# The step before the expert tiles of a two-layer attention and mixture-of-experts kernel: last batch's normalised rows on ScalarE, its statistics in two parts, two experts' weights sent between tile loads

## The reference

```
x = x + _L0_xattn_ref(_layernorm(x), ctx, ctx, ...)     # 16 heads, distance bias
x = x + _L0_ffn_ref(_layernorm(x), ...)                 # product keys, top 8, plus dense silu
x = x + _L1_xattn_ref(_layernorm(x), ctx, ctx, ...)     # 16 heads, relu projections
x = x + _L1_ffn_ref(_layernorm(x), ...)                 # below

def _L1_ffn_ref(x, ln_gamma, ln_beta, gate_w, w1, w2):  # E = 8 experts, K = 2, C = 256, F = 512
    mu, var = mean(xf), var(xf)
    rn = (xf - mu) * rsqrt(var + EPS) * ln_gamma + ln_beta
    probs = softmax(rn @ gate_w.T)
    rw, sel = top_k(probs, K)
    comb = sum(one_hot(sel, E) * rw[..., None], axis=1)
    h = gelu(einsum('nc,efc->enf', xf, w1))
    y = einsum('enf,ecf->enc', h, w2)
    return einsum('enc,ne->nc', y, comb)
```

## Time and profile before

| what | us |
|---|---|
| median of 3 runs | 1135.71 |
| lowest, highest | 1132.48, 1136.11 |
| profiled execution, its own time | 1129.27 |
| its span in the trace | 1127.5 |
| PE busy | 1001.2 (89%) |
| DVE busy | 783.4 (69%) |
| ACT busy | 652.5 (58%) |
| POOL busy | 497.7 (44%) |

### The profile page before, as it was taken

The page is one execution under the profiler, slowest core; times in us unless marked ns, Lnnn a source line. Parts: engine busy times, 40 slices in busy tenths (PEclk is TensorE's granted clock), DMA queues, the critical chain, the costliest instruction groups (busy, mean ns, idle before and its releaser), DMA issues.

```text
span 1127.5 us, 17009 instructions
## 1 busy us (share of the span) xinstructions
PE 1001.2 (89%) x5550; PEld 633.1 (56%) x5550; DVE 783.4 (69%) x1755; ACT 652.5 (58%) x874; POOL 497.7 (44%) x550
## 2 busy tenths in 40 slices
PE   8789999989778989989999779899998887999991
PEld 3345444434466778778777564344443333888881
DVE  7767688887888787787787346788888845344443
ACT  3356667666566766676677434576675560555550
POOL 6458898896415434433543342115051435122220
PEclk9899999999999999999999999999999889999996
DMA  8754979648999600000002231376554328222226
GB/s 245 224 171 161 289 194 354 192 156 267 230 220 217 124 1 1 1 2 0 1 6 74 62 104 54 112 209 150 149 148 121 96 81 342 62 70 71 71 62 224
DMA packets 74201, 149.89 MB, mean 133 GB/s; under 512 B 7823, under 2 KB 44577, under 8 KB 72580
## 3 DMA queue, kind: packets, MB, share of 16 engines
q1 hardware_dynamic: 61380, 98.80, 34.0%
q0 software_dynamic: 10800, 47.63, 11.9%
q10 hardware_dynamic: 1936, 2.36, 0.6%
HBM read 73.14 MB, written 76.25 MB: 133 GB/s over the span
## 4 chain that ended last, share of the span: by engine, by line
PE 63%; DVE 14%; ACT 10%; issue 5%; DMA 3%; POOL 3%; SPq 1%; ACTq 0%; DVEq 0%; POOLq 0%
PE ps L1313 15%; PE ps L1447 10%; PE ps L1428 7%; PE ps L1413 5%; PE ps L1387 4%; PE ps L1397 3%; PE ps L1655 3%; ACT pt L1105 3%; PE ps L1618 3%; PE ps L1632 3%; DVE negmax L1852 2%; PE ps L1776 2%; PE ps L1456 2%; PE ps L1331 1%; DVE moe_w L2198 1%
## 5 line engine op out<-in xcount | busy, mean ns | idle before, releaser
L1852 DVE TENSOR_REDUCE negmax<-ps 128x2 f32<-128x1024 f32 x256 | 309.7, 1222 | 60.2 <-PE ps L1413 58.2
L1105 ACT ACTIVATE pt<-ps 128x1024 f32<-128x1024 f32 x256 | 259.2, 1027 | 137.4 <-PE ps L1428 135.6
L1447 PE MATMUL ps<-pt,v_aug 128*32 128x512 f32 x1024 | 145.4, 634 | 3.9 <-POOL pt L804 3.1
L1428 PE MATMUL ps<-sq,sk 57*128 57x512 f32 (+1 forms) x512 | 129.2, 503 | 6.8 <-DMA sq<-m_sb 3.9
L1413 PE MATMUL ps<-sk,sq 56*128 56x512 f32 (+1 forms) x512 | 108.5, 429 | 18.8 <-ACT pt L1105 15.0
L804 POOL TENSOR_TENSOR pt<-pt,near 128x256 f32<-128x256 f32 x128 | 92.5, 730 | 51.0 <-ACT pt L1105 50.4
L1428 PEld LDWEIGHTS ps<-sq,sk 57*128 57x128 f32 (+1 forms) x512 | 49.4, 190 | 109.1 <-issue 71.0
L996 POOL DMA_INDIRECT expert_out<-yo,dest x39 | 38.1, 977 | 116.4 <-ACT yo L1280 101.7
L908 POOL TENSOR_TENSOR w_first<-w_first,moe_w 128x1024 f32<-128x1024 f32 x16 | 38.1, 2380 | 104.4 <-DVE pt L2190 103.6
L1618 PE MATMUL ps<-sel,hl 128*128 128x512 f32 x256 | 72.3, 415 | 5.1 <-DVE pt L2190 5.1
L1413 PEld LDWEIGHTS ps<-sk,sq 56*128 56x128 f32 (+1 forms) x512 | 50.5, 194 | 40.5 <-ACT pt L1105 28.4
(11 more groups left out here) (323 smaller groups left out, 2059.5 us busy)
## 6 DMA issues: line engine op xcount, KB each, us to landing
expert_rows<-zero SPq DMA_DIRECT2D x3, 5586.0 KB, 61.7
expert_weights_split<-wst POOLq DMA_DIRECT2D x8, 2048.0 KB, 8.5
qk_rows<-hl SPq DMA_DIRECT2D x30, 512.0 KB, 3.1
sk<-qk_rows SPq DMA_DIRECT2D x62, 192.0 KB, 5.0
sq<-qk_rows SPq DMA_DIRECT2D x62, 192.0 KB, 4.5
moe_w<-in_w POOLq DMA_DIRECT2D x16, 512.0 KB, 7.7
wexp<-expert_weights_split POOLq DMA_DIRECT2D x16, 512.0 KB, 4.8
wexp<-expert_weights_split SPq DMA_DIRECT2D x4, 2048.0 KB, 16.7
```

Source lines behind the costliest of these rows:

```text
L1105: act.activation(pt[:, 4 * (U % 2) + 2 * half:4 * (U % 2) + 2 * half + 2, :], ps[:, bank:bank + 2, :], ACT.Exp, scale=(BIAS, SCALE)[L]).th ...
L1428: ins = pe.matmul(ps[:, key.bank + s, :], sk[r, pair, c * P:(c + 1) * P], sq[r, pair, :], start=True, stop=True)
L1447: ins = pe.matmul(ps[32 * j:32 * j + 32, OBANK, :], v_aug[:, b % 2, c, HG * g + j, :], pt[:, 4 * (U % 2) + j, :], start=(c == 0), stop=(c ...
L1852: dve.tensor_reduce(negmax[:, n % 2, col:col + 9:8], ps[:, job.bank:job.bank + 2, :], AX, ALU.max, negate=True).then_inc(s_jd, 1)
```

## The change

Six edits.

1. In every batch `pick16`, which PE's ranking waits for, is made before the two small copies to `pay`, not after them.
2. For the last batch `gate_weights` stands in step 78, ahead of the places, and no longer in step 79 behind them.
3. The last batch's statistics are taken in two parts: 192 of 256 channels in step 64, once POOL has added the third group, and the last 64 channels where all 256 were. `bn_aggr` joins both.
4. The last batch's normalised rows are written by ACT (an activation with scale and bias per row) and not by POOL. DVE makes the bias, minus mean times inverse root, in `nb3`.
5. SP loads the weights of experts 4 and 5 where it loaded 4 to 7. Those of experts 6 and 7 go in quarters of 512 KB, two ahead of each of the row loads of tiles 3 to 6. The first row number is read before the wait for the sends.
6. PE's 14 filler products before the tiles become 12, then a wait for all sends, then 2.

```
             for e in (4, 5):
                 sp.dma_start(wexp[:, (ME - 1 - e) * EW:(ME - e) * EW].bitcast(F32), wx[e]).then_inc(s_wx[e], 16)
             sp.wait_ge(s_tile, 1)
-            for i in range(2):
-                sp.wait_ge(s_sent[i], 16 * 2 * TT * 2)
             for j in range(NTILE):
                 row = sp.value_load(tile_row[0:1, j:j + 1], min_val=0, max_val=XROWS - P)
+                if j == 0:
+                    for i in range(2):
+                        sp.wait_ge(s_sent[i], 16 * 2 * TT * 2)
+                if 3 <= j < 7:
+                    last_expert(6 + (j - 3) // 2, range(2) if j % 2 else range(2, 4))
                 if j >= 3:
...
                 if b == B - 1:
-                    norm3(b)
                     send_rows(b, range(TT))
...
+                        act.wait_ge(s_nb, 1)
+                        act.wait_ge(s_sent[(B - 1) % 2], 16 * 2 * TT)
+                        for t in range(TT):
+                            act.activation(pay[:, (B - 1) % 2, t, 0:D], x_tok[:, B - 1, t, :], ACT.Identity,
+                                           bias=nb3[:, t:t + 1], scale=rs3[:, 0, t:t + 1]).then_inc(s_ln3, 1)
...
-            keep_busy(14)
+            keep_busy(12)
+            for i in range(2):
+                pe.wait_ge(s_sent[i], 16 * 2 * TT * 2)
+            keep_busy(2)
...
+                    if L == 1 and U == LASTU:
+                        dve.wait_ge(s_res, NG * B - 1)
+                        stats_of(0, 64 * (NG - 1), 0, range(TT))
...
-                        if part == 12:
+                        if part == (11 if b == B - 1 else 12):
                             gate_weights(b)
...
                 for i in range(2):
                     own(dve.tensor_tensor(pick[:, i], per_e(col("expert")), per_t(two_e[:, i, :]), ALU.is_equal))
+                own.wait()
+                dve.tensor_tensor(pick16[:], pick[:, 0], pick[:, 1], ALU.add).then_inc(s_pick, 1)
+                if b == B - 1:
+                    dve.scalar_tensor_tensor(out=nb3[:], in0=mv3[:, :, 0], scalar=-1.0, in1=rs3[:, 0, :], op0=ALU.mult, op1=ALU.mult).then_inc(s_nb, 1)
                 if b >= 2:
                     dve.wait_ge(s_sent[b % 2], 16 * 2 * TT)
                 own(dve.tensor_copy(pay[:, b % 2, :, D + ME + 1], two_e[:, 0, :]))
                 own(dve.tensor_copy(pay[:, b % 2, :, D + ME], col("token")[:, TT * b:TT * (b + 1)]))
-                own.wait()
-                dve.tensor_tensor(pick16[:], pick[:, 0], pick[:, 1], ALU.add).then_inc(s_pick, 1)
```

More of the change, by code:

```diff
@@ L1761, in up @@
                 if j < ME:
-                    pe.wait_ge(s_wx[j], 16 if j >= 4 else 64)
+                    pe.wait_ge(s_wx[j], 16 if j in (4, 5) else 64)
                 pe.wait_ge(s_xl, j + 1)
@@ L1955, in attention @@
                             dve.wait_ge(s_res, NG * (b + 1))
-                            stats(0, x_tok[:, b], range(2 * part, 2 * part + 2))
+                            if b < B - 1:
+                                stats(0, x_tok[:, b], range(2 * part, 2 * part + 2))
+                            else:
+                                stats_of(64 * (NG - 1), D, 1, range(2 * part, 2 * part + 2))
                         if part == 1:
@@ L2043, in first_norm, with stats_of @@
                                       ALU.subtract, ALU.mult).then_inc(s_ln0, 1)
+            def stats_of(c0, c1, piece, blocks):
+                for t in blocks:
+                    own(dve.bn_stats(last6[:, t, piece, :], x_tok[:, B - 1, t, c0:c1]))
             def ln3_variance(b):
@@ L2047, in ln3_variance @@
                     dve.wait_ge(s_ln3, TT * b)
-                moments(0, mv3)
+                if b < B - 1:
+                    moments(0, mv3)
+                else:
+                    own.wait()
+                    for t in range(TT):
+                        own(dve.bn_aggr(mv3[:, t, :], last6[:, t].rearrange("p i s -> p (i s)")))
+                    own.wait()
                 own(dve.tensor_copy(vv[:, 0, :], mv3[:, :, 1]))
```

13 lines of the change are left out of this document (11 added, 2 removed).

## The result

| | before | after |
|---|---|---|
| median, us | 1135.74 (6 runs, 1132.48 to 1137.04) | 1126.65 (6 runs, 1120.38 to 1128.37) |
| ratio, 95% interval | | 0.9917 (0.9891 to 0.9943) |
| profiled execution, us (span) | 1129.27 (1127.5) | 1126.24 (1124.4) |
| granted clock, mean, profiled execution | 0.955 | 0.958 |

The two profiled executions are only 3.0 us apart. The median of before is 6.4 above its profiled execution, that of after 0.4 above its own. So there are two questions: what became of the terms on the path (5.0 forecast, 3.0 seen in the profiles), and where the other 6 us of the medians come from.

A forecast was written before the change was run, and what follows sets the result against it. PE's chain bounds, with a 32 us break between attention and tiles where one batch is finished, sent and fetched. 0.8 + 1.8 + 0.8 - 0.7 + 2.3 = 5.0 us; 1135.7 - 5.0 = 1130.7, range 1127.5 to 1134.0.

The forecast's parts named there:

- Tying the profiled execution to the median: Whole run: the median was 6.4 above the profiled 1129.27 us, and the like was expected of the changed kernel.
- `pick16` first, batches 0 to 2 (0.8): PE's waits for picks: `pick16`, held beside POOL's add, gains 0.28 us three times, 0.8 (0 to 2.2).
- First tiles' clock (2.3 won): First up products and the turn between: PE, busy from 952.5, regains full clock in time; 2.3 us won.
- Last two fillers (0.7 lost): After the sends land: two fillers take 3.00 us at half clock and delay the first turn; 0.7 lost (0 to 1.0).
- the clock does not come back: Rival, first tiles: fillers and first up products run at half clock; only 2.7 us gained, 1133.0 us; 22%.
- Last batch (1.8): Last batch, gate products to sends: faster DVE work and ACT's rows start the sends 1.8 us earlier (1.4 to 2.2).
- DVE's part: Last batch: norm off POOL ends DVE's stretched instructions, 1.45 us; `pick16` ahead of the two copies, 0.17.
- The weights' 0.6: Last batch: gate weights move into DVE's wait for PE's ranking, bringing row numbers 0.6 us earlier (0.4 to 0.6).
- ScalarE's duration: Last batch: four normalised rows on ACT take 2.0 us and, instead of DVE's row numbers, release the sends.
- SP (0.8 won): Last send to first row load: reading the row number before the wait saves 0.8 us (0.5 to 0.9).
- Weights between tiles: Experts 6 and 7's weights, sent between tile loads, land in about 5 us and cost nothing.
- Statistics in two parts: Last batch on DVE: at most 1.06 us goes, but costed at nothing since DVE waits for PE's gate products.

The follow-up runs named there:

- B: Comparison of kernels run on one chip beside the kernel before, testing addresses, repetition and fillers; before there: 1136.04 us, mean clock 0.9478.
- C: Comparison of kernels run on one chip beside the kernel before, testing which edit has the clock; before there: 1135.72 us, mean clock 0.947.
- a1: Kernel before with only `pick16` moved ahead of the two payload copies, in all four batches: 1131.36 us, ratio 1.0018.
- c3: Kernel before with only `pick16` ahead of the two copies in all batches, run again in another comparison: 1125.54 us, ratio 0.9920.
- b4: Changed kernel with the 14 fillers before the tiles in one go, as before: 1128.39 us, ratio 0.9941 to the kernel before.
- a2: Kernel before with only the last batch's normalised rows made by ScalarE (`nb3` added): 1134.45 us, ratio 1.0034.
- e1: Kernel before unaltered, run for a second profile: 1130.07 us, ratio 1.0015.
- d4: Changed kernel with one filler instead of three in the last ranking's step and one instead of two behind the last send: 1125.97 us, ratio 0.9920 to before.
- b1: Kernel before with one unused tile of 16 bytes per partition that shifts later addresses: 1134.65 us, ratio 1.0009.
- b2: Changed kernel with its two new tiles declared behind `dest`, so all others keep their old addresses: 1124.58 us, ratio 0.9895 to the kernel before.
- d2: Kernel before with `pick16` ahead of the two copies in batches 0, 2 and 3, not in batch 1: 1127.34 us, ratio 0.9933.
- e2: Kernel before with `pick16` ahead of the two copies in batch 0 alone: 1133.48 us, ratio 1.0036.
- c2: Changed kernel with `pick16` behind the two copies again in batches 0 to 2: 1136.44 us, ratio 1.0004 to the kernel before.
- A: Comparison of kernels run on one chip beside the kernel before, testing single parts of the change; before there: 1130.31 us, mean clock 0.9561.
- E: Comparison with the kernel before run once more and batch 0 alone; before there: 1129.32 us, mean clock 0.957, 2 of 23 executions under 0.950.
- a3: Kernel before with one unread product on PE ahead of its wait for the picks of batches 0 to 2: 1126.59 us, ratio 0.9962.
- c4: Changed kernel with new tiles behind `dest`, an unread product before batches 0 to 2's pick waits, and one filler for three and for two: 1119.88 us.
- d3: Kernel before with one unread product on PE ahead of its wait for batch 1's picks, nothing moved: 1125.69 us, ratio 0.9910.

## Why the prediction was wrong, step by step

**Tying the profiled execution to the median.** This step failed. Behind it lies a term that the sum does not have at all, the clock that PE loses behind batch 1's picks (next point). I made the sum against the profiled execution, found the median 6.4 us above it and expected the like of the changed kernel. The offset was no constant: after, it is 0.4. Three executions at 1132.48 to 1136.11 us beside a profiled one of 1129.27 say that the profile showed a luckier execution than most, and the fit says in what: 6.6 us for each 0.01 of granted clock. At equal clock after is 2.3 us faster than the before beside it in B and 0.9 in C, 2.0 with all comparisons pooled (1128.3 against 1130.2); the other 6 to 7 us of the medians are clock.

**`pick16` first, batches 0 to 2 (0.8).** On the path the term was right: PE stands 1.08, 1.08 and 1.33 us instead of 1.36, 1.35 and 1.60, 0.28 + 0.27 + 0.27 = 0.8 won. Whole runs can't resolve it: the same edit is worth 0.3 at equal clock in a1 and 2.3 in c3. What the step left out is that the half level followed batch 1's standstill in the profile of before, for ten us and 3.0 us of time. I read the clock only around the break. A view of the clock by stretch over the 100 us ahead of the first tile would have shown 0.50 from 872 to 882. The choice of 0.28 us a batch, against 0.7 with `pick16` not held, was my estimate from L2096 and L2080, and it was borne out (0.61 us for `pick16` beside POOL's add, 0.27 won); what the edit was worth lay beside it.

**First tiles' clock (2.3 won).** This term was wrong: the first up product takes 2.92 to 2.94, as before, in every kernel here, with 14 fillers together, 12 and 2, or 12 and 1. **Last two fillers (0.7 lost).** They take 3.75 us at a granted clock of 0.50, from 949.38 to 953.13, after PE idled 3.38, and the first turn comes 1.06 later than with 14 in one go (b4). I had read 3.00 for two at half clock, but the granted clock of that stretch, 927.34 to 930.34, is 0.59: the last part of them ran at the full level. The rival "the clock does not come back" was right about both. Its number for the profiled execution, 2.7 gained, is near the measured 3.0 by accident: 3.0 are batch 1's clock, 1.8 were there ahead of any changed instruction, 0.8 are the earlier picks and 0.3 the rest of the attention, 1.5 were lost in the break and 1.3 at the end.

**Last batch (1.8).** DVE's part is right against the profile that it was made from: 1.45 + 0.17 = 1.62 forecast from `gz` to `pick16`, 4.33 - 2.69 = 1.64 measured (1.48 in a2). Beside e1 it is 0.83: there only the shift of the four instructions is stretched (0.54), and product, cast and picks take 0.20, 0.17 and 0.29 with nothing changed and POOL's four instructions beside them. So the exact agreement is partly luck. The weights' 0.6 came too: 0.61 from the ranking to the row numbers. What was won ahead of the ranking was given back there, where it starts 2.08 behind `pick16` instead of 0.33 (1.10 in e1). I took it as following the picks, but DVE is now earlier than the three fillers that PE has ahead of it, and they run mostly at half clock (5.12 us at 0.55): the bound passed from DVE to PE. With one filler there it is 0.34 (d4). ScalarE's duration was right (2.07 for 2.0), but with the row numbers that late it is not what releases the sends.

**SP (0.8 won).** Right: 0.23 from landing to issue, 0.2 forecast. In after it is hidden behind the two fillers, since the turn waits for these. **Weights between tiles.** Right: never waited for; 4.9 us to landing, and a tile every 3.6 us in both. **Statistics in two parts.** At nothing, as forecast: DVE waits 3.29 us for PE's gate products.

**Left out: the addresses.** Two new tiles move all that are declared behind them. The results' fetching then lands in 7.8 instead of 6.8 us, and with eight of them one behind another the end is 1.3 longer; b1 and b2 put it at 1.4 and 1.7 at equal clock. The change would have been that much better with the tiles declared last, as b2 was.

**Open.** Why the half level lasts 10 us in one execution and 31 in another after the same standstill, what in batches 0, 2 and 3 kept d2 out of the lower group (e2 does not answer it), and why before meets it in four executions of five in one hour and hardly ever in another. There is no long stretch in a profile of before itself, only in c2's; that its lower group is the same thing is likely from the clock and not shown. The changed kernel was never run in an hour like A or E. From the levels at equal clock I would expect 1 to 2 us there and not 9 (an estimate); no run shows it.

## To carry to other kernels

Before an edit is summed on the critical path, list the granted clock by stretch over the whole kernel and look at each place where it falls behind a standstill of PE: in some hours a few tenths of a us on such a wait were worth 8 to 10 us and in others nothing, and one unread product in it did as much as the whole change. Compare the profiled execution with the other times of the same kernel before the sum is tied to either, and where they are apart, forecast each with its own clock. A second profile of the kernel before costs little and shows which of its pieces are clock. Declare new on-chip tiles behind the existing ones (ahead of them they cost 1.4 and 1.7 us at equal clock here), and after taking time from one engine in a chain, look again at what fills the time of the next one, since fillers placed for the old timing can become the bound (here the ranking began 2.08 us behind `pick16` instead of 0.33).

## What the runs showed of the hardware

- PE's standstills of 1.35 to 1.38 us for batch 1's picks were followed by the half clock (0.50) in six of eight profiles, for 3 to 31 us, those of 1.08 to 1.10 in one of nine. For batch 0's picks it followed 1.36 and 1.08 us alike, in all 18 profiles. The length of the standstill does not decide alone. A product that filled the wait kept the full clock behind it in all three profiles (batch 1: a3, c4, d3) and both (batch 0: a3, c4).
- The mean granted clock varied from 0.939 to 0.967 between the executions of the fit, at 6.6 us for each 0.01. The same kernel on the same chip had medians of 1135.72 and 1129.32 us in two comparisons.
- In ten us of the results' fetching, loads of 512 KB into `wexp`, the DMA engines moved 384 GB/s in before and 351 in b1, which differs only by an unused tile of 16 bytes per partition declared ahead of it, at a busy share of 1.09 in both.
- A VectorE instruction with two inputs in on-chip memory, 0.19 us by itself, took 0.61 beside POOL's add and ended within 0.05 us of it (after, batch 2).
